# A tile's denominator spread issued from ScalarE instead of SyncE, in a causal attention kernel

## What is computed

```python
x = x + attention(layernorm(x), W_qkv, W_out)   # x: 2 x 2048 x 256 fp32
x = x + ffn(layernorm(x), W, b, lora...)

# attention, 16 heads of 64, causal
score = einsum('bihd,bjhd->bijh', q, k) / 8
w     = softmax(masked score over j)
out   = einsum('bijh,bjhd->bihd', w, v) @ W_out
```

## Time and profile before

| | |
|---|---|
| runs | 1861.03 us median of 3 (1859.17 to 1866.96) |
| the profiled execution | 1860.62 us; its span 1858.8 us |
| granted TensorE clock | 0.996 of full |
| PE busy | 1774.3 us (95%) |
| DVE | 1243.1 us (67%) |
| POOL | 958.7 us (52%) |
| ACT | 788.2 us (42%) |
| DMA | 171.39 MB, 92 GB/s mean |

### The profile page before, as it was taken

How to read it: one execution, slowest core, us unless ns; L and a number is a source line. 1 busy time by engine, 2 the same in 40 slices (tenths; PEclk the granted TensorE clock), 3 DMA queues, 4 the chain that set the end, 5 groups by cost and what they waited for, 6 DMA issues and landing times. The chain is left out here.

```text
span 1858.8 us, 34889 instructions
## 1 busy us (share of the span) xinstructions
PE 1774.3 (95%) x13720; PEld 1051.1 (57%) x13720; DVE 1243.1 (67%) x2094; ACT 788.2 (42%) x982; POOL 958.7 (52%) x529
## 2 busy tenths in 40 slices
PE   7999999999999999999999999999999999999998
PEld 5878777554545454445454455445454545444897
DVE  5365653767676767676767767676767676756665
ACT  3222114454545454545454454545454545455231
POOL 1011001666665858485766656666667585835211
PEclk9999999999999999999999999999999999999999
DMA  5656446212121212122121222121212121022551
GB/s 209 223 184 233 164 176 215 69 42 75 47 69 48 72 50 69 47 69 73 49 70 47 78 59 78 41 81 36 81 47 70 47 75 47 24 75 92 193 204 57
DMA packets 153858, 171.39 MB, mean 92 GB/s; under 512 B 48202, under 2 KB 94816, under 8 KB 153696
## 3 DMA queue, kind: packets, MB, share of 16 engines
q1 hardware_dynamic: 153696, 169.17, 28.7%
HBM read 97.02 MB, written 71.57 MB: 91 GB/s over the span
## 5 line engine op out<-in xcount | busy, mean ns | idle before, releaser
L1047 DVE TENSOR_REDUCE f_part_max<-b_ring 128x1 f32<-128x512 f32 (+3 forms) x1200 | 675.0, 604 | 289.2 <-PE b_ring L872 193.3
L973 ACT ACTIVATE b_probs<-b_scores 128x1024 f32<-128x1024 f32 (+3 forms) x640 | 564.3, 898 | 604.0 <-PE b_scores L843 343.1
L1161 POOL TENSOR_TENSOR b_sum_pool<-b_sum_pool,b_probs 128x1024 f32<-128x1024 f32 x234 | 558.9, 2388 | 31.8 <-POOL b_sum_pool L1161 0.5
L843 PE MATMUL b_scores<-b_split 64*128 64x512 f32 (+2 forms) x1920 | 296.8, 418 | 0.0
L843 PE MATMUL b_scores<-f_split 64*128 64x512 f32 (+2 forms) x1920 | 295.9, 416 | 0.0
L1161 POOL TENSOR_TENSOR b_sum_pool<-b_probs 128x1024 f32<-128x1024 f32 x48 | 114.6, 2387 | 314.3 <-DVE g_sum_dve L1093 204.4
L908 PE MATMUL b_o_acc<-b_probs,b_v_in 128*64 128x512 f32 (+3 forms) x1280 | 271.2, 545 | 0.0
L908 PE MATMUL b_o_acc<-b_probs,f_v_in 128*64 128x512 f32 (+3 forms) x1280 | 269.0, 541 | 0.0
L843 PEld LDWEIGHTS b_scores<-b_split 64*128 64x128 f32 x1920 | 179.7, 189 | 12.0
L843 PEld LDWEIGHTS b_scores<-f_split 64*128 64x128 f32 x1920 | 179.5, 188 | 11.2
L1087 DVE TENSOR_TENSOR g_sum_dve<-g_sum_dve,b_probs 128x512 f32<-128x512 f32 (+3 forms) x198 | 158.1, 798 | 31.0 <-ACT b_probs L973 26.5
(11 more groups left out here) (138 smaller groups left out, 2208.8 us busy)
## 6 DMA issues: line engine op xcount, KB each, us to landing
f_raw<-k_t SPq DMA_DIRECT2D x32, 512.0 KB, 4.7
f_raw<-q_t SPq DMA_DIRECT2D x32, 512.0 KB, 5.8
g_recip<-r_t SPq DMA_DIRECT2D x128, 128.0 KB, 2.9
o_t<-g_o_norm SPq DMA_DIRECT2D x64, 256.0 KB, 2.0
q_t<-a_stage_a SPq DMA_DIRECT2D x32, 256.0 KB, 2.4
q_t<-a_stage_d SPq DMA_DIRECT2D x32, 256.0 KB, 2.0
k_t<-a_stage_a SPq DMA_DIRECT2D x32, 256.0 KB, 2.0
k_t<-a_stage_d SPq DMA_DIRECT2D x32, 256.0 KB, 2.0
```

What stands on the lines that cost most here:

```text
L843: last = nc.tensor.matmul(scores[s % 2][:, h, lo:TILE], a[u][head(h), keys], b[u][head(h), queries], start=False, stop=(term == 2 and not ...
L973: nc.scalar.activation(probs[s % PR][:, :, off:], scores[s % 2][:, :, off:], ACT.Exp, scale=scale).then_inc(exp_done, 1)
L1047: nc.vector.tensor_reduce(part_max[:, h, ib, c:c + 1], rowwise[h][:, 0:width], AX.X, ALU.max).then_inc(chunk_reduced, 1)
L1161: nc.gpsimd.tensor_tensor(sum_pool[:], first, probs[s % PR][:], ALU.add).then_inc(pool_added, 1)
```

## The change

The four spread DMAs leave SP's `invert` and are issued by ACT right behind its copy of the denominators. ACT first waits for its own copy to have been written, and for the reciprocal of the tile before, which reads `den_spread`. SP no longer waits for the copy. DVE's reciprocal gets a wait for the store of the tile before, which reads `recip_spread`; that order was kept by SP's own order until now.

```diff
                 def invert(n, t):
-                    wait_apart(sp, den_copied, n * TI + t + 2, o_stored, 1)
-                    for c in range(4):
-                        h, half = divmod(c, 2)
-                        sp.dma_start(den_spread[half * D:(half + 1) * D, h, :], den_row[c * P // 4:c * P // 4 + 1, :].rearrange(
-                            "o (p i) -> o p i", i=NB)).then_inc(den_moved, 16)
                     wait_apart(sp, inverted, n * TI + t + 1, o_stored, 1)
...
                     act.wait_ge(den_moved, (n * TI + t) * 64 + 1)
                     denom = ring[:, ring_banks["denom", t][0], 0:DEN]
                     nc.scalar.copy(den_row[:], denom).then_inc(den_copied, 1)
+                    act.wait_ge(den_copied, n * TI + t + 2)
+                    if n * TI + t:
+                        act.wait_ge(inverted, n * TI + t)
+                    for c in range(4):
+                        h, half = divmod(c, 2)
+                        act.dma_start(den_spread[half * D:(half + 1) * D, h, :], den_row[c * P // 4:c * P // 4 + 1, :].rearrange(
+                            "o (p i) -> o p i", i=NB)).then_inc(den_moved, 16)
...
                 def reciprocals(n, t):
                     dve.wait_ge(den_moved, (n * TI + t + 1) * 64 + 1)
+                    if n * TI + t:
+                        dve.wait_ge(inverse_stored, (n * TI + t) * 16)
                     nc.vector.reciprocal(recip_spread[:], den_spread[:]).then_inc(inverted, 1)
```

## The result

| | before | after |
|---|---|---|
| median of the runs, us | 1861.96 (4 runs) | 1890.47 (4 runs, 1890.26 to 1894.73) |
| ratio | | 1.0152, interval 1.0136 to 1.0169 |
| profiled execution, us; span | 1860.62; 1858.8 | 1894.73; 1892.9 |
| granted TensorE clock | 0.996 | 0.990 |

The kernel is 1.5% slower. The profiled execution of after is the longest of its four, 4.3 us above the median, and the one with the lowest clock (0.990; the other three have 0.993, 0.995 and 0.995).

A forecast was written before the change was run, and what follows sets the result against it. PE was taken to bound the kernel, busy 94.8 of 100 us. 1860.6 + 27.5 + 4 + 12 - 6.7 - 2 - 2.5 - 2.5 = 1890.4 us, range 1862 to 1904.

The forecast's parts named there:

- four issues hold ACT: Behind each copy of the denominators, ACT spends 2.43 us on its four issues, bounds 1.4 and 3.24.
- PE's waits at 14 boundaries: Behind the copies (n-1, 3) into items 1 to 14, PE waits 1.96 us each for exponentials: +27.5 us.
- clock behind them: Half of the 14 new boundary waits bring a stretch at half clock: +12 us, bounds 0 and +24.
- (n, 0): DVE's wait gone: At (n, 0) in items 0 to 14, DVE's 14 waits for late spreads go, counted in full: -6.7 us.
- (n, 1): Of DVE's 12.3 us of waits at (n, 1), only the excess over 0.7 reaches PE: -2 us, bounds 0 and -12.
- (n, 2): hidden: ACT's issues behind the copies (n, 2) fit into the room before PE needs the next exponential: cost 0.
- item 15: Three copies with dense work behind them cost +4 us (0 to 6); DVE's earlier sums give -2.5 (0 to -5).
- new wait of DVE for the store or of ACT for the reciprocal: Both added waits were put at 0; either showing in the profile after would be a sign against the prediction.
- rivals of cheaper and of costlier issues: Four issues hold ACT for 1.4 us, giving 1862 (chance 0.15), or for 3.24 us, giving 1916 (chance 0.14).
- two streams issuing at once: At (n, 0) SP issues two broadcasts with ACT; most of the spare 1.1 us would go, the sum hardly move.
- more issuing engines save only sequencer time: Skill sentence held against the change: removing SP's issues would be worth 0 and the sum 11 us higher.
- Cost 0 for 42 copies: Issues behind the copies (n, 0), (n, 1), (n, 2) are hidden from PE, even at 3.24 us for four.

The follow-up runs named there:

- the run of its own: ACT issues the spreads only behind the copies (n, 2), SP all others as in the kernel before: 1862.94 us, ratio 1.0010.
- The boundary alone: ACT issues the four spreads only behind the copies (n, 3), SP all others as in the kernel before: 1901.3 us, ratio 1.0227.
- t = 0 and 1 alone: ACT issues the spreads only behind the copies (n, 0) and (n, 1), SP the others as in the kernel before: 1846.09 us, ratio 0.9924.
- SP reordered: Kernel before with all spreads kept on SP, those of (n, 0), (n, 1) issued ahead of the store of the tile before: 1850.19 us, ratio 0.9945.
- an edit worth 8 to 10 us: SP places the next item's maxima ahead of the store of (n, 2); in the kernel before alone: 1849.38 us, ratio 0.9948.
- the profiles with two and three issues: Full change, but behind the copies (n, 3) ACT issues only two or three of the four spreads, SP the rest: 1858.64 and 1869.88 us.
- the placing moved: Full change, with SP placing the next item's maxima ahead of the store of (n, 2): 1874.41 us, ratio 1.0091.

## Why the prediction was right

Forecast 1890.4, measured 1890.47. So close an agreement is partly luck, since terms of several us were off both ways, and the clock's term fits the profiled execution (1894.7) better than those at the median. By its steps, against the profiled pair, which differs by 34.1 us:

| step | predicted | in the traces |
|---|---|---|
| four issues hold ACT | 2.43 us | 2.41 |
| PE's waits at 14 boundaries | +27.5 | +26.6 |
| clock behind them | +12, half of the 14 | +11.0, 7 of the 14 (and 0.8 in neither) |
| (n, 0): DVE's wait gone | -6.7 | -8.2 |
| (n, 1) | -2 | -1.6 |
| (n, 2): hidden | 0 | +6.8 in that execution, +1.7 in the run of its own |
| item 15 (+4, -2.5, and its part of the clock gained) | near 0 | -2.4 |
| rest (item 14, `project_and_ffn`) | 0 | +1.0 |

**What bounds the kernel.** Right: PE, and behind it one place per item. The boundary alone was enough for the loss, and t = 0 and 1 alone for a gain; each was run. No new wait of DVE for the store or of ACT for the reciprocal showed.

**The issue on ACT.** The step that had no row was priced from SP's rows at 2.43. That held, and so the rivals of cheaper and of costlier issues fell: ACT takes 618 ns for one where SP takes 589. The way that an issue could have become dearer by two streams issuing at once did not show on ACT. In the full change's trace 54 pairs of issues of ACT and SP overlap in time, and the median issue of ACT is 618 ns with and 617 without an overlap. It did show on SP where both issued spreads at once: at t = 3 with two and with one issue on ACT, SP's second issue usually takes 0.80 us, and 0.59 in the kernel before. The Trainium skill, in Perfetto Trace Analysis, section DMA Instruction — HWDGE, has such a wait for a shared generator as part of the window; SP's rows agree with it, and by ACT's rows it is too short to be seen there.

**The clock.** It was put at half of the boundaries from three old waits, with both ends kept. Half is what came in two traces (7 and 7 of 14), and 2 of 14 in a third. The unprofiled executions of the full change have a higher clock than its trace, so fewer stretches. That half came was luck in part, and the bounds were needed.

**What the removal gives.** Right in kind and near in size. The sentence of the Trainium skill (DMA: Bandwidth & Descriptors, section Issuing engines are not separate DMA queues), that more issuing engines save only sequencer time, holds here in this sense: SP reordered gives a ratio of 0.9945 without a second engine. What was saved was not SP's time but SP's place in the order.

**The step that failed** is "Cost 0 for 42 copies", at (n, 2). PE's exponentials had room, as argued. What was not followed is POOL behind them: "at 3.24 us for four they still cost nothing" looked at PE's next scores and not at the sums, the normalising and SP's placing. The runs showed 1.8 to 6.8 us there, a loss that the sum had no term for; it is small against the boundaries' term and did not decide the case.

## What to carry to other kernels

An issue of a DMA is an instruction of the queue that makes it, here 0.6 us each. On an engine that computes, look up at each place how long the next consumer can wait, since the mean busy share (ACT 42%) says nothing of it: 14 of 56 sets made the kernel slower, and of the other 42 only long ones at t = 2 cost time. Those left PE's next scores alone and reached PE over 20 us later, through POOL and SP's queue, so follow a delay through the other engines too. Before moving issues to another engine because a queue is late, see what the queue waits for, and try its own order first. And read the one-per-item waits of the bounding engine: the one under "issue", 6.8 us in all, led to an edit worth 8 to 10 us.

## What the runs showed of the hardware

**A long issue comes with an instruction fetch.** Some single issues take 0.9 to 2.6 us in place of 0.6 or less, on SP and ACT alike. In the kernel before, each of the 13 that took over 0.9 us in `attention` starts within 0.8 us of a packet of an instruction queue (q8), while only 91 packets of that queue fall in those 1400 us. But 27 other issues start as near to one and take 0.9 us or less, so a fetch nearby is not enough. In the trace of after it is 13 of 15. One case of after: the DMA queues from 1008.3 to 1010.2 us, then the timeline of ACT, whose last two issues fall there.

```profile
q8 instruction: 1, 0.02, 4.5%
q10 hardware_dynamic: 160, 0.00, 4.3%
```

```profile
1006.68 3.45 ACTq L1002 DMA_DIRECT2D g_den_spread<-g_den_row  x4
```

The packet moves 0.02 MB, and the set takes 3.45 us in place of 2.41. That the fetch delays the issue is inferred from this meeting in time; it was not tried.

**Waits and the lower clock.** At the boundaries, waits of PE of 0.62 and 1.26 us were followed by no stretch at 1.2 GHz (the profiles with two and three issues). Waits of 1.9 us were in 7 of 14 places in the full change, 7 with ACT at t = 3 alone, and 2 with the placing moved. One wait of 2.38 us, for the placed maxima in the run with two issues, was followed by one:

```profile
490.80:494.20 3.40, 3.26 (x24) 2.38 (x24) 0.14 (x1) 1.20 (x2) 0.00 (x0) 0.51 0.00 0
```

A wait of the same 2.38 us at the same place in the full change, at the start of item 2 (491.9 us), was not: from 490.4 to 493.4 us the clock is 1.00 there. In `project_and_ffn` of the kernel before, a half-clock stretch from 1728.8 us follows two waits of only 0.51 us with small products between them. So the length of one wait does not settle it. A stretch cost 1.55 us, the 11.34 against 9.79 us of the same 72 products.
